# Fewer waits per visit in the edge passes of a graph network, and one operation moved from VectorE to ScalarE

## The reference

```python
logits = leaky_relu(a_src[src] + a_dst[dst])      # gat (4 heads), typed (8 heads)
logits = sum(q[dst] * k[src], axis=-1) * scale    # attn (1 head)
m = segment_max(logits, dst, num_segments=n)
e = exp(logits - m[dst])
out = segment_sum(rows[src] * e, dst) / segment_sum(e, dst)
```

## Time and profile before

| | |
|---|---|
| median of 3 runs | 4923.0 us (4912.32 to 4923.89) |
| profiled execution, own time | 4959.05 us |
| its span | 4957.4 us |
| PE, DVE, POOL, ACT busy | 67%, 65%, 59%, 46% |
| mean granted TensorE clock | 0.788 of full speed |
| gathers issued: gat | 253.0 to 1484.1 us of the span |
| attn | 1729.5 to 3000.9 us |
| typed | 3231.2 to 4461.5 us |

### The profile page before, as it was taken

One profiled execution on the slowest core, in us unless ns is written; L12 is line 12 of the kernel. 1 busy time (PEld: TensorE's weight loads), 2 busy tenths in 40 slices (PEclk: granted clock), 3 DMA queues, 4 the chain that ended last, 5 costly groups with the idle time before them and its releaser, 6 DMA issues. The chain is left out here.

```text
span 4957.4 us, 74006 instructions
## 1 busy us (share of the span) xinstructions
PE 3333.3 (67%) x13766; PEld 2197.6 (44%) x13766; DVE 3239.2 (65%) x11427; ACT 2269.2 (46%) x6293; POOL 2911.1 (59%) x3158
## 2 busy tenths in 40 slices
PE   0536666766676657777777777836667666765998
PEld 0424444434443434444444444523444444434887
DVE  4546666666667946665656566847777777776665
ACT  0224555555553335555555555525545545553332
POOL 1266666666662456666666662366666666661776
PEclk9956766576668978898888889967676676677999
DMA  5345444544442334444434433544444444441221
GB/s 54 107 133 146 143 141 140 149 140 141 141 143 67 115 101 113 112 114 113 112 113 117 114 113 103 190 135 132 130 133 133 135 132 130 133 131 55 63 68 49
DMA packets 313472, 586.81 MB, mean 118 GB/s; under 512 B 106395, under 2 KB 204231, under 8 KB 313111
## 3 DMA queue, kind: packets, MB, share of 16 engines
q0 software_dynamic: 122944, 354.78, 26.1%
q1 hardware_dynamic: 147832, 188.48, 13.3%
q10 hardware_dynamic: 42336, 39.66, 2.3%
HBM read 504.91 MB, written 77.73 MB: 118 GB/s over the span
## 5 line engine op out<-in xcount | busy, mean ns | idle before, releaser
L561 PE MATMUL psum<-big,onehot 128*128 128x264 f32 (+2 forms) x4992 | 2149.5, 547 | 842.1 <-DVE big L733 312.8
L561 PEld LDWEIGHTS psum<-big,onehot 128*128 128x128 f32 x4992 | 1063.4, 253 | 1225.0 <-issue 675.2
L755 DVE TENSOR_TENSOR acc<-acc,psum 128x264 f32 (+2 forms) x2496 | 1051.3, 421 | 595.2 <-PE psum L561 372.0
L446 POOL DMA_INDIRECT big<-table_attn,tables x832 | 787.7, 947 | 499.8 <-PE psum L561 189.2
L446 POOL DMA_INDIRECT big<-table_gat,tables x832 | 841.1, 1011 | 403.8 <-issue 205.2
L446 POOL DMA_INDIRECT big<-table_typed,tables x832 | 816.7, 982 | 429.5 <-issue 215.3
L472 ACT ACTIVATE dist<-iota,tables 128x128 f32<-128x128 f32 x2496 | 1000.0, 401 | 101.2 <-DMA tables<-edge_tables 14.3
L484 ACT ACTIVATE onehot<-dist,ones 128x128 f32<-128x128 f32 x1664 | 649.6, 391 | 854.1 <-PE psum L561 552.5
L518 PE MATMUL psum<-big,onehot_t 128*128 x2496 | 484.6, 308 | 239.0 <-issue 144.7
L597 DVE CUSTOM_DVE_ANT_0 junk<-psum,big 128x258 f32<-128x258 f32 x832 | 344.6, 415 | 323.7 <-DMA joins<-visit_joins 174.4
L481 ACT ACTIVATE onehot<-dist,weight,neg_weight 128x128 f32<-128x128 f32 x832 | 400.4, 482 | 318.9 <-PE psum L561 184.4
(11 more groups left out here) (251 smaller groups left out, 3625.9 us busy)
## 6 DMA issues: line engine op xcount, KB each, us to landing
onehot_t<-onehots SPq DMA_DIRECT2D x104, 512.0 KB
big<-visit_positions SPq DMA_DIRECT2D x52, 512.0 KB
onehots<-onehot_t SPq DMA_DIRECT2D x52, 512.0 KB
seg<-visit_segments SPq DMA_DIRECT2D x676, 24.1 KB
big<-table_gat,tables POOLq DMA_INDIRECT x832
big<-table_attn,tables POOLq DMA_INDIRECT x832
big<-table_typed,tables POOLq DMA_INDIRECT x832
big<-in_x_dram SPq DMA_DIRECT2D x98, 128.0 KB
```

What stands on the lines that cost most here:

```text
L446: pool.indirect_dma_start(X[:, v % RING, :], None, ph.table, bass.IndirectOffsetOnAxis(ap=column(k, 0)[:, g:g + 1].bitcast(I32), axis=0)). ...
L561: nc.tensor.matmul(sum_ps(v), m.onehot[:, v % 4, :], X[:, v % RING, 0:ph.WS], start=True, stop=True).then_inc(S["summed"], 1)
L755: nc.vector.tensor_tensor(row, row, sum_ps(v), ALU.add).then_inc(S["added"], 1)
```

## The change

Distance, one-hot, main matmul and add each keep one wait in the common case. In gat and typed, distance v waits for the scaling of v; in attn for the add of v - 4 (from v = 4 on). One-hot v waits for distance v alone, the main matmul for one-hot v alone (in attn the last visit also for an add). Distance is issued one visit ahead of one-hot instead of three. The scaling of v gets a wait of its own, for the add of v - 4. The add keeps its wait for the add before only in attn and in the last visits. In attn, dot waits for gathered rows once in four visits and no longer for the dot before the last; `junk` has three buffers. `m.onehot` and `m.dist` become two halves of one tensor. In gat the transposed one-hots are made on ACT by two activations (Abs in place, then Relu with scale -1 and bias 1), at the same v, at the end of ACT's iteration.

```diff
--- before.py
+++ after.py
@@ -373,6 +373,10 @@
     def column(k, a):
         return m.tables[:, k % TB, a * G:(a + 1) * G]
 
+    def onehot_at(v):
+
+        return m.onehots[:, v % 4, :]
+
     def rows_at(k):
         at = k * G % RING
         return X[:, at:at + G, :]
@@ -465,34 +469,46 @@
 
             def distance(v):
                 k, g = divmod(v, G)
-                if g == 0:
+                if g == 0 and ph.dot:
                     act.wait_ge(S[f"tables{k % TB}"], (k // TB + 1) * 16)
-                if v >= 4:
-                    act.wait_ge(S["onehot"], v - 3)
+                if not ph.dot:
+                    act.wait_ge(S["scaled"], v + 1)
+                elif v >= SB + 1:
+                    act.wait_ge(S["added"], v - SB)
                 nc.scalar.activation(m.dist[:, v % 4, :], m.iota[:, :], ACT.Abs, scale=-1.0,
                                      bias=column(k, 1)[:, g:g + 1]).then_inc(S["distance"], 1)
 
             def onehot(v):
                 k, g = divmod(v, G)
                 act.wait_ge(S["distance"], v + 1)
-                if v >= 4:
-                    act.wait_ge(S["summed"], v - 3)
                 if ph.dot:
-                    nc.scalar.activation(m.onehot[:, v % 4, :], m.dist[:, v % 4, :], ACT.Relu,
+                    nc.scalar.activation(m.onehots[:, v % 4, :], m.dist[:, v % 4, :], ACT.Relu,
                                          scale=m.neg_weight[:, k % 2, g:g + 1], bias=m.weight[:, k % 2, g:g + 1]).then_inc(S["onehot"], 1)
                 else:
-                    nc.scalar.activation(m.onehot[:, v % 4, :], m.dist[:, v % 4, :], ACT.Relu,
+                    nc.scalar.activation(m.onehots[:, v % 4, :], m.dist[:, v % 4, :], ACT.Relu,
                                          scale=-1.0, bias=m.ones[:, 0:1]).then_inc(S["onehot"], 1)
 
+            def transposed_onehot(k):
+                act.wait_ge(S[f"positions{k % 2}"], (k // 2 + 1) * 16)
+                at = m.rel_row.bitcast(BF16)[:, k % 2, :]
+                nc.scalar.activation(at, at, ACT.Abs, scale=-1.0, bias=m.pcol[:, 0:1]).then_inc(S["spacing"], 1)
+                act.wait_ge(S["spacing"], k + 1)
+                if k >= 2:
+                    act.wait_ge(S["expanded"], k - 1)
+                    act.wait_ge(S[f"onehot_stored{k % 2}"], k // 2 * 16)
+                nc.scalar.activation(m.onehot_t[:, k % 2, :], at, ACT.Relu, scale=-1.0, bias=m.ones[:, 0:1]).then_inc(S["onehot_t"], 1)
+
             weigh_at = G - 1 if ph.dot else G - 2
-            for v in range(-LEAD, VISIT_END):
-                if 0 <= v + 3 < VISIT_END and v + 3 >= 0:
-                    distance(v + 3)
+            for v in range(-3 * G, VISIT_END):
+                if 0 <= v + 1 < VISIT_END:
+                    distance(v + 1)
                 if v >= 0:
                     onehot(v)
                 k, g = batch_at(v)
                 if k is not None and g == weigh_at:
                     weigh(k)
+                if ph.name == "gat" and v % G == 2 and 0 <= v // G + 2 < NBATCH:
+                    transposed_onehot(v // G + 2)
 
         @block.tensor
         def _(pe):
@@ -554,11 +570,9 @@
                             expand(u + i, blks[(u + i) % 4])
                 if v >= 0:
                     pe.wait_ge(S["onehot"], v + 1)
-                    if not ph.dot:
-                        pe.wait_ge(S["scaled"], v + 1)
-                    if v >= SB:
+                    if ph.dot and v == VISIT_END - 1:
                         pe.wait_ge(S["added"], v + 1 - SB)
-                    nc.tensor.matmul(sum_ps(v), m.onehot[:, v % 4, :], X[:, v % RING, 0:ph.WS], start=True, stop=True).then_inc(S["summed"], 1)
+                    nc.tensor.matmul(sum_ps(v), onehot_at(v), X[:, v % RING, 0:ph.WS], start=True, stop=True).then_inc(S["summed"], 1)
                 k, g = batch_at(v)
                 if k is not None:
                     if g == ph.masked_at + 2:
@@ -579,22 +593,13 @@
                     m.blocks[0:1, k * G:(k + 1) * G], engines=[DVE_ENGINE], min_val=0, max_val=NB - 1,
                     skip_runtime_bounds_check_because="visits() keeps them within the blocks")[1]
 
-            def transposed_onehot(k):
-                dve.wait_ge(S[f"positions{k % 2}"], (k // 2 + 1) * 16)
-                if k >= 2:
-                    dve.wait_ge(S["expanded"], k - 1)
-                    dve.wait_ge(S[f"onehot_stored{k % 2}"], k // 2 * 16)
-                nc.vector.tensor_scalar(m.onehot_t[:, k % 2, :], m.rel_row.bitcast(BF16)[:, k % 2, :],
-                                        m.pcol[:, 0:1], None, ALU.is_equal).then_inc(S["onehot_t"], 1)
-
             def dot(v):
                 dve.wait_ge(S["expanded"], v + 1)
-                landed(dve, v)
-                if v >= 2:
-                    dve.wait_ge(S["dotted"], v - 1)
+                if v % QUARTER == 0:
+                    landed(dve, v)
                 if v % G == 0 and v:
                     dve.wait_ge(S["logits"], v // G)
-                nc.vector.tensor_tensor_reduce(out=m.junk[:, v % 2, 0:K], in0=ps[:, exp_banks[v % 3], 0:K], in1=X[:, v % RING, 0:K], scale=1.0,
+                nc.vector.tensor_tensor_reduce(out=m.junk[:, v % 3, 0:K], in0=ps[:, exp_banks[v % 3], 0:K], in1=X[:, v % RING, 0:K], scale=1.0,
                                                scalar=0.0, op0=ALU.mult, op1=ALU.add,
                                                accum_out=m.raw[:, v % G:v % G + 1]).then_inc(S["dotted"], 1)
 
@@ -728,6 +733,8 @@
                         dve.wait_ge(S["edge_scale"], k + 1)
                     else:
                         dve.wait_ge(S["weights"], k + 1)
+                if v >= 4:
+                    dve.wait_ge(S["added"], v - 3)
                 row = X[:, v % RING, 0:D].rearrange("p (h c) -> p h c", h=H)
                 w = m.edge_scale[:, g, 0:H] if ph.typed else X[:, v % RING, D:D + H]
                 nc.vector.tensor_tensor(row, row, spread(w, D // H), ALU.mult).then_inc(S["scaled"], 1)
@@ -749,7 +756,7 @@
                 dve.wait_ge(S["summed"], v + 1)
                 if v % G == 0:
                     dve.wait_ge(S["rescaled"], v // G + 1)
-                else:
+                elif ph.dot or v >= VISIT_END - 3:
                     dve.wait_ge(S["added"], v)
                 row = m.acc[:, bass.ds(blk * WA, ph.WS)]
                 nc.vector.tensor_tensor(row, row, sum_ps(v), ALU.add).then_inc(S["added"], 1)
@@ -774,8 +781,6 @@
                     scale_rows(v + 2)
                 if ph.dot and 0 <= v + DOT_AHEAD < VISIT_END:
                     dot(v + DOT_AHEAD)
-                if ph.name == "gat" and v % G == 2 and 0 <= v // G + 2 < NBATCH:
-                    transposed_onehot(v // G + 2)
                 k, g = batch_at(v)
                 for at, place, part in parts:
                     if k is not None and (at, place) == (g, 0):
@@ -1725,7 +1730,8 @@
         m.first_hot, m.cont = sb("first_hot", [P, NBATCH]), sb("cont", [P, NBATCH])
         m.tables, m.seg, m.joins = sb("tables", [P, TB, A * G]), sb("seg", [P, 2, SEG]), sb("joins", [P, 2, 4 * 2 * G])
         m.onehot_t = sb("onehot_t", [P, 2, G * P], BF16)
-        m.onehot, m.dist = sb("onehot", [P, 4, P]), sb("dist", [P, 4, P])
+        m.onehots = sb("onehots_or_distances", [P, 8, P])
+        m.dist = m.onehots[:, 4:8, :]
         m.raw, m.logit, m.shifted = sb("raw", [P, P]), sb("logit", [P, P]), sb("shifted", [P, P])
         m.ahead, m.local, m.with_first, m.seg_max = sb("ahead", [P, P]), sb("local", [P, P]), sb("with_first", [P, P]), sb("seg_max", [P, P])
         m.ends, m.ends_t = sb("ends", [P, 64]), sb("ends_t", [P, 64])
@@ -1734,7 +1740,7 @@
         m.grown, m.growth, m.shrink = sb("grown", [P, 1]), sb("growth", [P, HB]), sb("shrink", [P, HB])
         m.both, m.edge_scale = sb("both", [P, G, 2 * HB]), sb("edge_scale", [P, G, HB])
         m.weight, m.neg_weight = sb("weight", [P, 2, G]), sb("neg_weight", [P, 2, G])
-        m.junk = sb("junk", [P, 2, WQ])
+        m.junk = sb("junk", [P, 3, WQ])
         m.psum = ctx.enter_context(nc.psum_tensor("psum", [P, 8, 512], F32))
 
         constants(nc, m)

```

## The result

The changed kernel takes 4987.4 us (median of 4 runs, 4982.2 to 4997.8), the kernel before 4922.2 us in the same comparison: a ratio of 1.0144, 95% interval 1.0125 to 1.0163. The direction was right (slower), the size was not: +65 us where +637 us was forecast, and 4987 stands at the low end of the range. So the two profiles by themselves understate the difference.

The account below looks back on a forecast made before the run. It took a ring of waits around the main matmul, not the gathers, as the bound. 387 + 30 + 111 + 109 = +637 us on 4959 gave 5596, less 36 for the runs' median 5560 us; range 4980 to 6200 us.

Parts of the forecast that it names:

- M: Time from the scaled row until the same visit's add begins: in gat and typed 5.19 us before, 3.57 forecast.
- the lap: One round of the ring of waits: in gat and typed 5.94 us over four visits, forecast 5.20 over three.
- Gat and typed chain: Three visits for four in the lap, with two more ACT instructions: +0.25 us a visit, +387 us.
- Tails: Last 48 visits of gat and typed, after the last gather, at 1.19 us for 0.88: +30 us.
- Attn: In attn, distance behind an earlier add lengthens the lap: half of +222 us taken, nothing if hidden in M.
- ACT block: Gat's transposed one-hots on ACT, 3.85 us a batch, 2.1 of it counted, 52 times: +109 us.
- Removed waits: Fewer waits on PE and DVE: 0 us taken, 127 us if PE's queue is the limit.
- The section on SBUF's sides: Gat's bf16 compare on DVE may hold up POOL's descriptors; moving it could give 64 ns a gather, 53 us.
- D: Rival for the whole kernel: nothing changes, because gains of C and losses of B meet; chance 0.04.
- B: Rival: gathers plus a fixed pause pace the ring; gat and typed +116 us, ACT block about +70; about 5110; chance 0.21.
- A: Rival: M doesn't shrink at all; +1686 us, about 6600 us; chance 0.14.
- C: Rival: PE's queue is the limit, so fewer waits make the kernel faster, 4760 us; chance 0.11.

Follow-up runs that it names:

- e1: The kernel before with only the first ring of gathers issued in each pass, first chip: 3782.8 us, where the kernel before takes 4446.7 us.
- e7: The kernel before with three PSUM banks instead of four in gat and typed: 4976.1 us, where the kernel before takes 4971.7 us.
- e11: The changed kernel, unaltered, on a fourth chip: 4983.0 us, 1.0141 of the kernel before.
- e14: The changed kernel with the transposed one-hots on DVE and only the first ring of gathers issued in each pass: 4122.0 us, one run.
- e4: The changed kernel with the transposed one-hots back on DVE, on the first chip: 4414.4 us, 0.9918 of the kernel before.
- e9: The same kernel as e4 on a slower chip: 4977.0 us, 1.0014 of the kernel before.
- e5: The kernel before, unaltered, run again on a third chip: 4921.2 us in one run.
- e6: The changed kernel, unaltered, run beside e5 on the third chip: 4988.3 us, 1.0146 of the kernel before.
- e12: The changed kernel with the transposed one-hots on ACT in eight pieces, one a visit, a batch earlier: 4924.8 us, 1.0022 of the kernel before.
- e3: The kernel before with only the transposed one-hots moved to ACT, all waits as before, first chip: 4429.7 us, 0.996 of the kernel before.
- e10: The same kernel as e3 on a slower chip: 4979.1 us, 1.0014 of the kernel before.
- e2: The changed kernel with only the first ring of gathers issued in each pass: 4191.9 us.
- e8: The kernel before with gather v waiting for the add of v - 48 instead of its matmul: 5112.0 us, 1.0288 of the kernel before.

## Why the prediction was right in direction and wrong in size

**The bound.** The step that failed is M. The prediction took the time that a visit spends between its scaled row and its add (5.19 us) as a cost of the lap, divided the lap by the visits in the ring, and kept 3.57 of it in the new one by a choice in the middle of two ends 3.2 us apart; the sum hung on it. M was mostly slack. With the gathers gone the same ring turns in 0.94 to 1.11 us a visit on the first chip (e1); with three banks for four the pace stays and the time shrinks (e7); and in the changed kernel the mean time from a visit's weight load to its add fell in gat from 4.44 to 2.05 us, in typed from 4.45 to 2.45. Put in the forecast's lap (1.63 us and M, over three) these would give 1.23 and 1.36 us a visit, under the old pace, where 1.73 was forecast and 1.54 and 1.46 measured: the longer chain hides, but for the block.

What the prediction said of the gathers, that they are not what is late, holds for a chip of the slower kind, where POOL is 44 to 47 visits ahead in gat; on the first chip they are what is late. On both kinds their being there slows the passes: attn, with the same code and on one chip, goes at 1.49 us a visit in e11 and at 0.955 in e14. One signal was read wrongly as well: in the earlier trace rows POOL starts at 949.48, 3.1 us behind the one-hot and the add of 946.4, so it was not one signal of PE that let all three go.

**Gat and typed chain, +387 us.** With gathers it is worth nothing that can be told (e4 0.9918, e9 1.0014), the typed pass +7.4 us in the pair e5, e6. The chain itself was priced too high as well: without gathers +0.16 us a visit in gat (e14 less e1, on two chips, whose rates for attn and typed agree without gathers) and +0.13 in typed, where the forecast had +0.25.

**Tails, +30 us.** After the last gather there is no cover, and the forecast's price is about right. Adds of gat, attn, typed after the last gather, to be held against the earlier trace rows:

```profile
1526.90:1582.00 55.10, 20.12 (x48) 0.82 0.06 15
3036.20:3071.00 34.80, 16.59 (x40) 1.00 0.05 9
4479.40:4534.00 54.60, 20.83 (x48) 0.84 0.04 7
```

The last gat gather began 54 us before the last add (before: 40 us), in typed 54 us (before: 45): some +22 us of the foretold 30.

**Attn, +111 us.** Nothing: -8.7 us in the pair e5, e6, and even without gathers 0.955 for 0.940 us a visit. The new chain did hide in M, the end of the range that the forecast named and did not take.

**ACT block, +109 us.** The durations were right: 1.986 and 2.002 us for the 1.90 estimated, and 2.0 by the figures of the Trainium skill ("ScalarE: Activation LUTs", section "Rules for kernel authors"), with which this trace agrees. The cost on the path came to about 60 us (changed kernel less e9's or e12's ratio, 1.2 to 1.3% of 4920), a little over half of the forecast. The advice of that section of the Trainium skill, such functions belong on VectorE, turned out right for this kernel, but not by the operation's own price: on the old waits the 4 us cost nothing (e3, e10), with distances three visits ahead and ACT idle beside them.

**Removed waits, 0.** Confirmed within what can be told on one chip (e9); on the first the new waits alone gave 0.8%. Of the 2485 instructions of L560, 1656 hold two waits each, so a visit of gat or typed lost one instruction for two waits.

**The section on SBUF's sides.** The move of the bf16 compare was to give POOL 64 ns a gather. The gat gathers take 986 ns after and 1011 in the earlier trace rows; in e9, with the compare still on DVE, 987, and in e10, with the old waits and the compare moved, 989. So either part alone gives the 25 ns, and the 64 were not there to be had. The gathers that run while the compare does are longer, though: 72 of them take 1138 ns in the kernel before, the other 760 take 999; in e4 it is 1245 ns for 55 and 973 for the rest. That agrees with the rule of the Trainium skill that the prediction cites ("SBUF — State Buffer", section "SBUF: two separate sides"), but other work of DVE stands beside them too, and in the kernel before it comes to 10 us of POOL's time in all.

**The rivals.** In the total D (nothing changes, about 4923 us) was nearest, then B (5110). B had attn's nothing and about the block's price (70 us for some 60), and gat at 1.56 us a visit (measured 1.54), but that last is luck: it came from a fixed pause of 0.94 us spread over three visits for four, and by it gat in e7 and typed in the changed kernel should stand at 1.56 too, where they measure 1.49 and 1.46. A and C fell. The text's own test, "if gat rises much more than typed, ACT's block is dearer than I think", pointed to the cause, though it is dear only in company: a lead of three visits had covered it, and the other part of the change took the lead away.

## What to carry to other kernels

Before pricing a longer chain, ask how fast the chain turns without the transfers beside it; one run with only the first ring of gathers says it, and here a chain that stayed under the transfers' 1.25 us cost nothing. The time that a visit spends in a ring is no measure of its path: when rings have slack, it grows to fill the buffers. A long operation on an engine costs what the lead of that engine's output doesn't cover: shortening the lead and adding the long operation can each be free and together not, so price them together. Where such an operation must stand in a chain, cut it in pieces, one a visit, even if the pieces add up to more.

## What the runs showed of the hardware that was not expected

The same kernel takes 4447 us on one chip and 4912, 4912 and 4972 us on three others, and most of the difference lies in the edge passes (487 us of 545 between e3 and e10, one kernel on two chips): without gathers attn and typed run at the same rate on two of them (0.955 and 1.240 us a visit in e2 and e14, a chip of each kind). On the slower kind the counter that a main matmul raises seems to come late while gathers run. In the kernel before, 128 adds of gat begin after DVE stood idle for over 0.15 us, in the median 4.2 us after the recorded end of their matmul (which is modelled); in the changed kernel 183 do, the median at 0.15 us and the longest tenth above 3.15. Without gathers it is 0.15 us for all 55 of e2. By the counter's own record, the first change behind a matmul of the changed kernel's gat comes 0.9 us after its end in the median and 3.9 at the 90th percentile; but that trace holds only 502 of the 832 changes, so these two are too high by an unknown amount. In e14, on a chip of the slower kind, and in e4, on the fast one with gathers, the record of gat has all 832 and the delay is 0.01 us. The counters of ACT and DVE are not late: in gat of the changed kernel and of e4 nine in ten distances that waited for their scaling start within 0.04 us of its end, and nine in ten weight loads within 0.05 us of their one-hot's.

Whether this delay is what makes the slower chips slow is not shown. It is not most of the forecast's M: the kernel of e3 and e10 takes 3.66 us from weight load to add in gat on the fast chip and 3.84 on a slower one, and in e4 on the fast chip the counter is on time. What delays it is open. It is not POOL's own wait on the matmul's counter: in e8 POOL waits for the add, and the delay stays (1.25 us in the median in gat, by the record of 613 changes).

It is open, too, why v % 16 = 2 is a worse place for the block than v % 16 = 12. And no version here is shown to beat both kernels on every chip: the new waits with the compare left on DVE are 0.8% faster on the first chip and the same as before on another, and the changed kernel has no time on the first.
